# Order of the transfers in SP's queue: the maxima rows ahead of the value products and of the reciprocal's round trip

## The reference, cut to what matters

```
q = layernorm(x) @ Wq + bq;  k, v = source @ Wk + bk, source @ Wv + bv
scores = q @ k.T * scale (+ mask);   p = softmax(scores);   a = p @ v
x = x + a @ Wo + bo
```

## Time and profile before

| | |
|---|---|
| runs | 4698.58, 4701.06, 4720.01 us; median 4701.06 us |
| the profiled execution | 4725.3 us, its span 4723.6 us (1.7 us lie around it) |
| mean granted TensorE clock | 0.923 of full speed |
| busy: TensorE / VectorE / ScalarE / GpSimd | 4283.3 (91%) / 2568.7 (54%) / 2255.5 (48%) / 1317.2 us (28%) |
| DMAs on SP's queue | 135152 packets, 216.02 MB, 22.7% of 16 engines' span |

### The profile page before, as it was taken

The page is one execution under the profiler, slowest core; times in us unless marked ns, Lnnn a source line. Parts: engine busy times, 40 slices in busy tenths (PEclk is TensorE's granted clock), DMA queues, the critical chain, the costliest instruction groups (busy, mean ns, idle before and its releaser), DMA issues. The chain is left out here.

```text
span 4723.6 us, 63401 instructions
## 1 busy us (share of the span) xinstructions
PE 4283.3 (91%) x20306; PEld 2058.4 (44%) x20306; DVE 2568.7 (54%) x6513; ACT 2255.5 (48%) x4789; POOL 1317.2 (28%) x1405
## 2 busy tenths in 40 slices
PE   6888899999797899999999999999798899999998
PEld 3333333333464333333444443333266455555555
DVE  4555557776013677777777776777211344444443
ACT  2444446666221566654444446666321455555554
POOL 2222221110221011111111111111121566566664
PEclk7888789999897899999999999999699999999999
DMA  4322334443001444333222224343100000000000
GB/s 92 77 58 59 59 60 92 75 77 53 19 0 29 95 77 74 66 55 67 48 47 45 47 48 91 74 71 70 39 0 22 10 1 10 10 10 10 10 6 10
DMA packets 135466, 219.93 MB, mean 47 GB/s; under 512 B 42736, under 2 KB 45168, under 8 KB 133488
## 3 DMA queue, kind: packets, MB, share of 16 engines
q1 hardware_dynamic: 135152, 216.02, 22.7%
HBM read 59.69 MB, written 5.51 MB: 14 GB/s over the span
## 5 line engine op out<-in xcount | busy, mean ns | idle before, releaser
L937 ACT ACTIVATE Pr<-ST 128x512 f32<-128x512 f32 (+3 forms) x2560 | 1339.8, 565 | 1355.1 <-PE ST L510 930.4
L510 PE MATMUL ST<-stk 50*128 50x512 f32 (+3 forms) x2560 | 1076.3, 478 | 94.1 <-ACT Pr L937 81.0
L1132 DVE TENSOR_REDUCE mx<-MX 128x1 f32<-128x512 f32 x1056 | 702.7, 684 | 359.7 <-PE MX L510 357.7
L510 PE MATMUL MX<-stk 48*128 48x512 f32 (+3 forms) x1760 | 745.9, 464 | 162.2 <-DMA stk<-mrows 139.4
L510 PE MATMUL OV<-Pr,V 128*32 128x512 f32 (+3 forms) x5120 | 713.7, 633 | 2.5 <-ACT Pr L937 1.5
L1487 POOL TENSOR_SCALAR Pr<-Pr,mx 128x128 f32<-128x128 f32 (+3 forms) x512 | 548.4, 1083 | 384.8 <-DVE mx L1270 384.8
L510 PEld LDWEIGHTS MX<-stk 48*128 48x128 f32 x1760 | 320.3, 199 | 710.2 <-issue 353.7
L510 PEld LDWEIGHTS ST<-stk 50*128 50x128 f32 x2560 | 447.3, 199 | 313.4 <-ACT Pr L937 274.9
L1384 POOL CAST mhl<-mx 128x16 fp32r<-128x16 f32 x160 | 31.4, 196 | 1650.4 <-DVE mx L1132 1079.2
L510 PE MATMUL OV<-stk 48*128 48x512 f32 (+3 forms) x800 | 364.4, 455 | 6.1 <-DVE mx L1132 5.8
L1132 DVE TENSOR_REDUCE mx<-OV 128x1 f32<-128x512 f32 x480 | 326.5, 680 | 60.6 <-PE OV L510 60.4
(11 more groups left out here) (137 smaller groups left out, 6802.6 us busy)
## 6 DMA issues: line engine op xcount, KB each, us to landing
stk<-hi SPq DMA_DIRECT2D x640, 128.0 KB, 3.8
stk<-lo SPq DMA_DIRECT2D x320, 128.0 KB, 3.9
misc<-misc SPq DMA_DIRECT2D x160, 128.0 KB
sums<-spread SPq DMA_DIRECT2D x80, 256.0 KB
misc<-in_ctx_t SPq DMA_DIRECT2D x24, 512.0 KB, 5.2
W_even<-in_w SPq DMA_DIRECT2D x4, 1024.0 KB, 5.2
W_even<-in_w SPq DMA_DIRECT2D x2, 2048.0 KB, 10.7
XH<-in_ctx_rows SPq DMA_DIRECT2D x8, 512.0 KB, 4.3
```

The source lines that it names most:

```text
L510: return nc.tensor.matmul(o, l, r, start=start, stop=stop)
L937: nc.scalar.activation(Pr[:, i % 2, h, q0:S], ST[h % 2][:, q0:S], ACT.Exp).then_inc(ex_done, 1)
L1132: nc.vector.tensor_reduce(m, bank[:, :], AX.X, ALU.max).then_inc(mx_red, 1)
```

## The change

Two lines of SP's slot move; no instruction is added or removed, and all waits stay with their DMAs. `max_rows` of group 1 goes ahead of `spread_rows`, and `max_rows` of the next unit's group 0 goes ahead of `move` of group 0.

```
--- before.py
+++ after.py
@@ -391,10 +391,10 @@
                             stack(U + 1, 1 - half, 1, GB + half, kind)
                     if on["tail"]:
                         move(U - 1, 1 - half, 1, GB - 1 + half)
-                        spread_rows(U - 1, 1 - half)
                     if on["b"]:
                         max_rows(U, half, 1)
                     if on["tail"]:
+                        spread_rows(U - 1, 1 - half)
                         widen(U - 1, 1 - half)
                     if cross and half == 0 and 0 <= b < NB - 2:
                         sp.wait_ge(lb_full, JOBS * (GB + 1))
@@ -402,10 +402,10 @@
                     if on["a"]:
                         for kind in range(2):
                             stack(U + 2, half, 0, GB + 1, kind)
+                    if on["m"]:
+                        max_rows(U + 1, 1 - half, 0)
                     if on["b"]:
                         move(U, half, 0, GB)
-                    if on["m"]:
-                        max_rows(U + 1, 1 - half, 0)
```

## The result

The changed kernel takes 4586.4 us (median of 4 runs, 4574.6 to 4589.6), the kernel before 4710.5 us (median of 4 runs, 4698.6 to 4724.3: the three of the table and a fourth): ratio 0.973 (95% interval 0.969 to 0.977), 124 us less. The forecast was 4508 us with a range up to 4565. The gain has the right sign; it is 60% of the sum of 208 us. The result lies 21 us above the range. One run of a later kernel (the kernel before with the later reciprocal) took 5774.0 us at a mean clock of 0.644 and is left out of that kernel's median.

What follows compares the result with a forecast made beforehand. TensorE, 91% busy, was taken as the bound, stalled by 38 late maxima rows. 146.6 + 44 + 9 + 8 = 208 us off gave 4517 (profiled execution) or 4493 (median); forecast between them 4508 us, range 4475 to 4565.

Steps and rivals of the forecast that it cites:

- the sum of 208 us: Whole kernel: 146.6 us of stall plus clock gains of 44 (cross stages), 9 (SELF2) and 8 us (SELF0).
- The stall and its cause: At half 0 to half 1 borders, TensorE's 38 waits for the maxima row, queued behind `move` held by `op_full`: 146.6 us.
- The clock: After each stall the clock dips; both go: 44 us in the cross stages, 9 in SELF2, 8 in SELF0.
- The rival that the dips stay: The stall goes but half clock remains: 147 us gained, 4554 us; chance 0.11.
- a sign of that rival: In the profile after: cross stages' clock still 0.95 to 0.97 with no stall, then 4554 us.
- part one: At the slot border, the row of group 0 goes ahead of `move`: all 38 waits go, 146.6 us.
- What `move` loses: in half 0 slots nothing: `move` waits for `op_full` as before; the stack of group 1 starts 0.8 us sooner against it; cost 0.
- Is anything else late at 1906.45?: At the example border in CROSS1: stack landed by 1900.4, VectorE ended at 1905.76, nothing else late; all 38 waits counted.
- another wait takes part of its place: Likeliest the stack of group 1 at (4, 0), or DVE or ACT in self stages: 76 us back, 4584 us; chance 0.07.
- Part two: In SP's queue, the row of group 1 goes ahead of `spread_rows`: no gain in TensorE's waits, cost 0.

Runs made afterwards that it cites:

- the later reciprocal: VectorE's reciprocal moved from position (1, 3) to (2, 3): in the changed kernel 4480.1 us, 0.951; in the kernel before 4746.1 us, 1.005.
- the full stall: Against the kernel before: row of group 1 ahead of `spread_rows`, reciprocal at (2, 3), `move` still ahead of the row of group 0: 4714.7 us, 0.9995.
- with none: The changed kernel, both rows moved ahead, with the reciprocal at (2, 3) instead of (1, 3): 4480.1 us, 0.951.

## Why the prediction was wrong

*The stall and its cause.* Right. 38 waits, all for the row behind `op_full`, all gone.

*The clock.* Right in kind, and for the cross stages in size. Between the kernels with the full stall and with none (both with the later reciprocal), from the first to the last row copy of a stage, the cross stages differ by 43.4, 39.2 and 49.4 us; less 23 stalls of 3.86 us, that leaves 43 us, against 44 predicted. The self stages were sized too low: SELF2 51.5 less 8 stalls = 21 us (9 predicted), SELF0 46.4 less 7 stalls = 19 us (8 predicted). Of SELF2's 21 us, 9 lie at the borders, as predicted, and 12 inside the half 0 slots: the stall also brought the slow stretches in the middle of the batch, which I had left out. SELF2's clock is 0.95 with the stall and 1.00 without, where I had counted only the 41 of 73 us that start at a stall. The rival that the dips stay holds for SELF0 alone, at 0.88 without any stall. With the changed kernel as it stands CROSS1 was still at 0.97, which I had set down as a sign of that rival; it is at 0.99 once the reciprocal comes later, so there the new waits kept it low. The Trainium skill's penalty ("TensorE: Matmul & The Clock Gate", Terms) of half of the throttled time gave 54 us for the cross stages; the 43 measured agree with the rows and not with it.

*The sum.* 208 us was forecast for part one with nothing in the way, 235 us were measured in that case; of the 27 us more, 23 lie in the two self stages.

*The step that failed* is in part one: "What `move` loses: in half 0 slots nothing", and "Is anything else late at 1906.45?", answered for the border only. I looked at what TensorE needs at the border and at the stack of group 1 at (4, 0). I did not look at what stands behind that stack in the same burst: `move` of group 1, whose sums VectorE wants at (1, 3), before (4, 0). That the reciprocal reads what `move` brings is in the text, but only for the half 1 slots' `move`. The stall had been the cover: it held TensorE and VectorE while SP's queue and the DMA engines drained after `op_full`. SP's start after `op_full` didn't move, the engines' did. With the trace of before the price could have been estimated: the sums out at 1915.69 and, if they land 1.4 us later like the DMA in the earlier trace rows, there by 1917.1; the reciprocal at 1918.81, so 1.7 us of cover, against engines that come 3.9 + 1.4 us sooner and a queue that comes 0.8 us sooner: some 3 us short. The changed kernel shows 2.98, though by another road: the sums go out 3.4 us sooner after `move` than before (5.7 us, from 9.1), and VectorE has them only 4.7 us later. The half 0 slots of before had shown both halves of this, 4.6 us behind the stack and a wait of 1.42 us where no stall gave cover. It was not in all 38 slots either: the eight of SELF2 have no such wait. The experiments put the price at 106 us (part of it clock), of which 74 us show as longer half 1 slots. The rival "another wait takes part of its place" had the right size, 4584 us, by luck: it named the wrong wait and was given 7 in 100.

*Part two.* Right: 0 by itself. Once the reciprocal comes later it takes away 29 waits, 15 us.

What keeps SELF0's clock at 0.88 without any stall stays open, and whether a still later or differently placed `move` would raise it wasn't tried.

## What to carry to other kernels

A stall is also a cover: when it goes, every engine arrives sooner except the one that was held by something else, here the queue behind `op_full`. After pricing the stall, list everything that the late queue still has to bring, in order, with the place at which each engine waits for it, not only what the stalled engine needs next. And a wait on an engine off the path is worth a look before the change: VectorE's 1.4 us for the sums, in the half 0 slots where no stall went ahead, showed what would be late in the half 1 slots without theirs.

## What the runs showed of the hardware

The sums are 8 KB. When they land is not in the trace, only when VectorE goes on: 4.7 us after the issue behind the burst (932.97 to 937.70), 4.6 us in a half 0 slot of the kernel before (946.29 to 950.92). The DMA of the reciprocals, twice as large and with no burst ahead, landed in 1.4 us. SP issues `move` and six stack DMAs, 0.9 MB, within 5 us of `op_full`, and the next `move` with the sums right behind. The 16 DMA engines are then busy for 6 us, though their mean over the span is 24% (the last three columns: clock, DMA share, GB/s; a share can pass 1 because each packet is counted where it starts):

```profile
928.50:930.50 2.00, 2.00 (x12) 0.65 (x8) 2.00 (x5) 1.49 (x4) 0.00 (x0) 1.00 0.39 133
930.50:932.50 2.00, 2.00 (x15) 0.69 (x14) 2.00 (x5) 1.46 (x3) 0.00 (x0) 1.00 1.06 154
932.50:934.50 2.00, 2.00 (x8) 0.81 (x10) 2.00 (x8) 1.08 (x2) 1.31 (x3) 1.00 1.08 117
934.50:936.50 2.00, 2.00 (x18) 0.53 (x14) 0.21 (x1) 1.65 (x3) 1.92 (x2) 1.00 0.99 114
936.50:937.70 1.20, 0.40 (x2) 0.08 (x2) 0.00 (x1) 1.18 (x3) 1.20 (x1) 1.00 0.03 2
```

VectorE goes on about a microsecond after the engines fall idle. So here a small late DMA waited twice, for its issue and, as these rows suggest, for the transfers ahead of it. The mean DMA share shows nothing of such a burst.
